# Linear attention with a feed-forward layer: the numerators' state part as 32x32 tiles, and the fourth denominators in the next group

## The reference

```python
def step(carry, qkv_t):
    kv_s, k_s = carry
    q_t, k_t, v_t = qkv_t
    kv_s = kv_s + jnp.einsum('bhe,bhf->bhef', k_t, v_t)
    k_s = k_s + k_t
    num = jnp.einsum('bhe,bhef->bhf', q_t, kv_s)
    den = jnp.einsum('bhe,bhe->bh', q_t, k_s)[..., None] + EPS_DEN
    return ((kv_s, k_s), num / den)
...
h = _layernorm(x, axis=-1) * (1 + ca) + sa
x = x + ga * _L0_attn_ref(h, L0_attn_W_qkv, L0_attn_b_qkv, L0_attn_W_out, L0_attn_b_out)
h = _layernorm(x, axis=-1) * (1 + cb) + sb
x = x + gb * _L0_ffn_ref(h, L0_ffn_w_gate, L0_ffn_w_up, L0_ffn_w_down)
```

## Time and profile before

| | us |
|---|---|
| median of 3 runs | 2108.07 |
| lowest, highest | 2107.64, 2109.33 |
| the profiled execution | 2109.39 |
| span of its instructions | 2107.6 |
| mean granted TensorE clock | 0.994 |

### The profile page before, as it was taken

How to read it: one execution, slowest core, us unless ns; L and a number is a source line. 1 busy time by engine, 2 the same in 40 slices (tenths; PEclk the granted TensorE clock), 3 DMA queues, 4 the chain that set the end, 5 groups by cost and what they waited for, 6 DMA issues and landing times. The chain is left out here.

```text
span 2107.6 us, 41310 instructions
## 1 busy us (share of the span) xinstructions
PE 2055.4 (98%) x14832; PEld 1669.0 (79%) x14832; DVE 1581.5 (75%) x2152; ACT 1006.0 (48%) x1733; POOL 991.0 (47%) x790
## 2 busy tenths in 40 slices
PE   5999999999999999999989999999999999999999
PEld 4788888888888888888868878788887888878787
DVE  7988988989989889889785674757557575674744
ACT  5444454455544555444434643535455354643533
POOL 2635545555454465544454344444434444344444
PEclk9999999999999999999999999999999999999999
DMA  7011122221232222222156465554656546465543
GB/s 254 31 52 58 65 86 86 96 91 56 78 99 81 91 68 79 86 81 80 65 171 229 153 220 170 193 181 145 209 179 199 179 153 211 153 219 170 168 157 109
DMA packets 157150, 276.60 MB, mean 131 GB/s; under 512 B 11105, under 2 KB 35681, under 8 KB 157026
## 3 DMA queue, kind: packets, MB, share of 16 engines
q1 hardware_dynamic: 156498, 273.73, 39.4%
q10 hardware_dynamic: 528, 1.05, 0.1%
HBM read 208.67 MB, written 66.06 MB: 130 GB/s over the span
## 5 line engine op out<-in xcount | busy, mean ns | idle before, releaser
L1429 POOL TENSOR_TENSOR h_lo<-y_rows,h_hi 128x512 fp32r<-128x512 f32 x192 | 246.7, 1304 | 406.9 <-ACT h_hi L1530 406.9
L424 POOL TENSOR_TENSOR x_res<-y,x_res 128x512 f32<-128x512 f32 x64 | 82.2, 1284 | 302.0 <-DVE y L843 302.0
L820 DVE RECIPROCAL r_den<-r_den 128x512 f32<-128x512 f32 x64 | 213.7, 3340 | 0.0
L582 ACT ACTIVATE z_exp<-pj,qk_neg 128x512 f32<-128x512 f32 x128 | 88.2, 689 | 213.9 <-PE pj L1073 186.6
L1073 PE MATMUL pj<-xt_hi,w_hi 128*128 128x512 f32 x512 | 151.0, 416 | 8.7 <-ACT xt_hi L574 4.2
L825 DVE TENSOR_TENSOR probs<-sc,causal 128x512 f32<-128x512 f32 x256 | 158.3, 678 | 1.3 <-PE sc L1101 1.3
L1836 PE MATMUL sc<-wd,h_hi 128*128 128x512 f32 x384 | 151.9, 396 | 5.7 <-DVE y L1666 5.7
L1836 PE MATMUL sc<-wd,h_lo 128*128 128x512 f32 x384 | 149.7, 390 | 0.0
L1642 DVE TENSOR_TENSOR r_den<-pj,k_tok 128x512 f32<-128x512 f32 x96 | 66.2, 689 | 103.5 <-ACT k_tok L1513 54.6
L1073 PE MATMUL pj<-xt_lo,w_hi 128*128 128x512 f32 x512 | 140.2, 396 | 0.9 <-DVE xt_lo L792 0.9
L1073 PE MATMUL pj<-xt_hi,w_lo 128*128 128x512 f32 x512 | 138.3, 392 | 0.0
(11 more groups left out here) (252 smaller groups left out, 5643.9 us busy)
## 6 DMA issues: line engine op xcount, KB each, us to landing
w_hi<-parts SPq DMA_DIRECT2D x48, 1024.0 KB, 5.2
w_lo<-parts SPq DMA_DIRECT2D x48, 1024.0 KB, 5.2
x_mid<-x_res SPq DMA_DIRECT2D x96, 256.0 KB, 2.1
x_res<-in_L_attn_x SPq DMA_DIRECT2D x64, 256.0 KB, 3.0
xg<-in_L_attn_x SPq DMA_DIRECT2D x15, 1024.0 KB, 6.9
x_res<-x_mid SPq DMA_DIRECT2D x60, 256.0 KB, 3.8
full<-x_mid SPq DMA_DIRECT2D x60, 256.0 KB, 3.3
parts<-r_den SPq DMA_DIRECT2D x48, 256.0 KB, 2.3
```

The lines of the kernel that those rows point to most:

```text
L424: pool.tensor_tensor(out=x_res[:, slot, :], in0=y[:, :], in1=x_res[:, slot, :], op=ALU.add).then_inc(y_ready, 1)
L582: act.activation(z_exp[:, n % 2, :], pj[:, n % 2, :], ACT.Relu, bias=qk_neg[:, 1 - kind, c:c + 1], scale=-scale).then_inc(below_ready, 1)
L820: dve.reciprocal(r_den[parity][:, c, :], r_den[parity][:, c, :]).then_inc(rden_ready, 1)
L1429: pool.tensor_tensor(out=h_lo[b], in0=h[i], in1=h_hi[b].bitcast(F32), op=ALU.subtract).then_inc(h_lo_ready, 1)
```

## The change

Three things change.

1. The state part becomes 16 products of 32x32, one for each head and block, which read only the nonzero blocks. The tile's row position is its head's partitions. Even blocks write their own head's partitions of `num`; odd blocks write one head further, in another bank: a bank of `sc` already masked (bank 3 in tiles 0 and 1, bank 2 in tiles 2 and 3, bank 0 in the last group). The V part writes to the same places. The division is two instructions of half width, one from each bank. Features of odd blocks so lie one head further from here on: the denominators use a second matrix `head_ones[:, 1, :]`, and the rows of W_out are put in the same order on the host.
2. The next group's denominator 3 no longer stands in tile 3 behind the numerators, but in the next group, between the first and the second projection unit of tile 0. ACT's copy of it goes behind the first `exp_relu`, and the vector engine's reciprocal behind the first `feature`. Denominator 1 moves ahead of the output projection in tile 2. In group 14 denominator 3 stands at the end of tile 3.
3. The waits follow: the scores wait for the division of the tile before, the numerators for the masks and copies of the bank that they borrow.

```diff
+    def odd_scores(tile, t):
+        return 0 if isinstance(tile, int) and tile >= (NG - 1) * GT else (3, 3, 2, 2)[t]
+    def num_part(tile, t, c, h):
+        to = (h + c % 2) % HPC
+        bank = sc[:, odd_scores(tile, t), :] if c % 2 else num
+        return bank[to * E:(to + 1) * E, c * P:(c + 1) * P]
...
             if ahead:
                 exp_relu(n, 0)
+                if not isinstance(g, int) or g > 0:
+                    den_out(g, parity, 3, den_bank)
                 exp_relu(n, 1)
...
-                exp_relu(n, 7)
                 if not isinstance(g, int):
                     act.wait_ge(down_out, g * 16 + (-16))
                 den_out(n, other, 1, den_bank)
+                exp_relu(n, 7)
...
-            if ahead:
-                den_out(n, other, 3, den_bank)
             if two_ahead:
                 xt_full(g + 2, 3, x_bank)
                 xt_high(g + 2, parity, 3)
+            if isinstance(g, int) and g == NG - 2:
+                den_out(n, other, 3, den_bank)
...
-            dve.tensor_tensor(out=a_t[:, :].rearrange("p (c i) -> p c i", c=C),
-                              in0=num[:, :].rearrange("p (c i) -> p c i", c=C),
-                              in1=r_den[parity][:, :, t * P:(t + 1) * P], op=ALU.mult).then_inc(a_ready, 1)
+            for odd, bank in enumerate((num, sc[:, odd_scores(tile, t), :])):
+                ins = dve.tensor_tensor(out=a_t[:, :].rearrange("p (k e i) -> p e k i", e=2, k=2)[:, odd, :, :],
+                                        in0=bank[:, :].rearrange("p (k e i) -> p e k i", e=2, k=2)[:, odd, :, :],
...
+            ins.then_inc(a_ready, 1)
...
             mask(g * GT)
+            if ahead:
+                feature(n, other, 0)
             recip(g, parity, 3)
-            if ahead:
-                feature(n, other, 0)
...
             wait(pe, y_gated, tile - 1)
+            wait(pe, a_ready, tile)
             wait(pe, ktok_ready, tile)
...
             wait(pe, kv_ready, tile)
-            wait(pe, a_ready, tile)
+            wait(pe, probs_ready, tile * HPC + odd_scores(tile, t) + 1)
+            if t >= 2 and (not isinstance(g, int) or g + 1 < NG):
+                wait(pe, den_ready, (g + 1) * C + t)
             for c in range(C):
-                pe.matmul(num[:, c * P:(c + 1) * P], kv_diag[:, c, :], qt[parity][:, c, t * P:(t + 1) * P],
-                          start=(c == 0), stop=False, skip_group_check=True)
+                for h in range(HPC):
+                    rows = slice(h * E, (h + 1) * E)
+                    pe.matmul(num_part(tile, t, c, h), kv_diag[rows, c, rows], qt[parity][rows, c, t * P:(t + 1) * P],
+                              start=(c < 2), stop=False, skip_group_check=True)
...
             if ahead:
                 project(g + 1, 1 - parity, 3 * t)
+                if t == 0 and (not isinstance(g, int) or g > 0):
+                    wait(pe, probs_ready, g * GT * HPC + 3)
+                    denominators(g, 3, den_bank)
                 project(g + 1, 1 - parity, 3 * t + 1)
...
-            if t == 3 and ahead:
+            if t >= 2 and ahead:
                 wait(pe, probs_ready, tile * HPC + 3)
-                denominators(g + 1, 2, den_bank)
+                denominators(g + 1, t - 1, den_bank)
...
-            if t == 3 and ahead:
-                denominators(g + 1, 3, den_bank)
...
+            if isinstance(g, int) and g == NG - 2 and t == 3:
+                pe.wait_ge(a_ready, tile + 1)
+                denominators(g + 1, 3, den_bank)
```

More of the change, by code:

```diff
@@ L124, in build @@
         causal = sbuf(top, "causal", [P, P])
-        head_diag = sbuf(top, "head_diag", [P, P])
-        head_ones = sbuf(top, "head_ones", [P, P], F32R)
+        head_ones = sbuf(top, "head_ones", [P, 2, P], F32R)
         c_col = sbuf(top, "c_col", [P, C])
@@ L876, in vector @@
         dve.memset(half_neg[:, :], -0.5)
-        link(dve.memset(head_diag[:, :], 0.0))
-        for h in range(HPC):
-            ins = dve.memset(head_diag[h * E:(h + 1) * E, h * E:(h + 1) * E], 1.0)
+        same_head = junk[:, 0:2 * P].rearrange("p (e n) -> p e n", e=2)
+        link(dve.memset(same_head, 0.0))
+        for odd in range(2):
+            for h in range(HPC):
+                to = (h + odd) % HPC
+                ins = dve.memset(same_head[h * E:(h + 1) * E, odd, to * E:(to + 1) * E], 1.0)
         link(ins)
-        dve.tensor_copy(head_ones[:, :], head_diag[:, :])
+        link(dve.tensor_copy(head_ones[:, :, :], same_head))
         dve.memset(ones[:, :], 1.0)
@@ L956, in group @@
                 dve.wait_ge(beyond_ps, 1)
-                dve.tensor_scalar(wide[:, :], x_bank[0:1, 0:1], 0.5, None, ALU.is_gt).then_inc(wide_ready, 1)
+                dve.tensor_scalar(wide[:, :], den_bank[0:1, 0:1], 0.5, None, ALU.is_gt).then_inc(wide_ready, 1)
             if ahead:
@@ L1079, in denominators @@
             wait(pe, den_ready, g * C + c)
-            pe.matmul(bank, head_ones[:, :], prod_hi[:, :], start=True, stop=False)
-            pe.matmul(bank, head_ones[:, :], prod_lo[:, :], start=False, stop=True).then_inc(den_ps, 1)
+            pe.matmul(bank, head_ones[:, c % 2, :], prod_hi[:, :], start=True, stop=False)
+            pe.matmul(bank, head_ones[:, c % 2, :], prod_lo[:, :], start=False, stop=True).then_inc(den_ps, 1)
         def scores(tile, g, parity, t):
@@ L1087, in scores @@
             wait(pe, y_gated, tile - 1)
+            wait(pe, a_ready, tile)
             wait(pe, ktok_ready, tile)
-            if not isinstance(g, int) or g + 1 < NG:
-                wait(pe, den_ready, (g + 1) * C + (0, 0, 1, 2)[t])
+            if not isinstance(g, int) or g > 0:
+                if not isinstance(g, int) or g + 1 < NG:
+                    wait(pe, den_ready, (g + 1) * C + t - 1)
+                else:
+                    pe.wait_ge(den_ready, NG * C)
+            else:
+                pe.wait_ge(den_ready, C + max(t - 1, 0))
             if isinstance(tile, int) and tile == (NG - 2) * GT + 1:
@@ L1124, in numerators @@
                     f = c * P + h * E
-                    mm = pe.matmul(num[h * E:(h + 1) * E, c * P:(c + 1) * P], v[parity][:, t, f:f + E],
-                                   probs[:, h, c * P:(c + 1) * P], start=False, stop=(c == C - 1),
+                    mm = pe.matmul(num_part(tile, t, c, h), v[parity][:, t, f:f + E],
+                                   probs[:, h, c * P:(c + 1) * P], start=False, stop=(c >= 2),
                                    skip_group_check=True)
@@ L1203, in rest @@
                 out_project(tile - 1)
-            if t in (1, 2) and ahead:
+            if t == 1 and ahead:
                 wait(pe, probs_ready, tile * HPC + 3)
-                denominators(g + 1, t - 1, den_bank)
+                denominators(g + 1, 0, den_bank)
             if t >= 2 and (not isinstance(g, int) or g + 2 <= NG):
@@ L1214, in rest @@
                 pe.wait_ge(probs_ready, (tile + 1) * HPC)
-                pe.matmul(x_bank[0:1, 0:1], beyond[:, :], ones[:, :], start=True, stop=True).then_inc(beyond_ps, 1)
+                pe.wait_ge(den_ready, (NG - 1) * C)
+                pe.matmul(den_bank[0:1, 0:1], beyond[:, :], ones[:, :], start=True, stop=True).then_inc(beyond_ps, 1)
             if isinstance(tile, int) and tile == 0:
@@ L1941 @@
             a = a.reshape(C, P)
+        if name == "L0_attn_W_out":
+            a = a.reshape(C // 2, 2, HPC, E, D)
+            a = np.stack([a[:, 0], np.roll(a[:, 1], 1, axis=1)], axis=1).reshape(D, D)
         layouts = [(f"in_{name}", a.T if name in _TURNED else a)]
```

9 lines of the change are left out of this document (6 added, 3 removed).

## The result

The changed kernel takes 2140.69 us, the median of four executions (2137.93 to 2142.56), the kernel before on the same chip 2108.23. The ratio is 1.0153, with an interval from 1.0141 to 1.0165: slower by 32.5 us. The forecast was 2140. Of all executions behind this document one, of `e8_full_matmuls`, stands apart (2548.70 us at a mean granted clock of 0.754, where its five others have 0.995 to 0.997); the numbers leave it out.

The account below looks back on a forecast made before the run. TensorE, busy for 98% of the span, was taken as the bound. Terms of -18.6, +2.2, -8.0, +36.7, +2.1 and +0.4 made +14.8 us, the clock +17, together +32: 2140 us against the median 2108.07, range 2110 to 2155.

Parts of the forecast that it names:

- State part: Numerators' state part as 32x32 tiles: four bursts, 0.69 us instead of 0.98, -18.6 us over 64 tiles.
- (c): State part: the two blocks of small tiles don't overlap, 2169 us, or in part 2150; chance 0.09.
- (d): State part: row tiles queue for the PSUM bank, +1.1 us a tile, 2229 us; chance 0.03.
- V part: Numerators' V part: columns turned by one head for odd blocks make bursts start later, 0.035 us a tile, +2.2 us.
- Fourth denominator out of tile 3: Between V part and x transposes in tile 3: 0.57 us saved a group, -8.0 us over 14 groups.
- The wait: Moved denominator in next group's tile 0 waits 2.5 us for the third mask: +2.62 a group, +36.7 us.
- Second denominator: Ahead of tile 2's output projection: waits about 0.15 us for the third mask, +2.1 us over 14 groups.
- Sum without the clock: Whole kernel: all terms except the falls of the granted clock sum to +14.8 us.
- The last group: Last group's waits for divisions and for the copy of the last denominator ahead of the first scores: +0.4 us once.
- The clock: Behind the denominator's stop: the granted clock falls in 10 of 14 groups, 1.7 us each, +17 us.
- Rival (b): Border: vector engine ahead of GpSimd, wait 1.7 us, clock holds, shape changes free: 2099 us; chance of faster 0.10.

Follow-up runs that it names:

- e8_full_matmuls: Kernel before, with the fourth denominator moved behind the next group's first unit and, except for the last group, the third reciprocal behind the masks: 2100.34 us.
- e1_move_alone: Kernel before, with only the fourth denominator, its copy and its reciprocal moved behind the next group's first unit, no small tiles: 2156.96 us.
- e6_tiles_one_bank: Kernel before, with the state part as 32x32 tiles in their natural places, both feature blocks in bank `num`: 2113.28 us, ratio 1.0029.

## Why the prediction was right, step by step

**State part: right.** Priced at 0.69 instead of 0.98, four bursts and two changes of shape; measured 0.59 and 0.10 ahead (scores to state part in tile 1 is 10.40 us for 10.30). -0.29, as said. The rivals on its size, (c) and (d), are out: no burst of one block waited for the other, and no row tile for its bank.

**V part: the term should have been nothing.** I took +0.035 us a tile for the turned columns. The V part's starts span 0.808 us as before; 2.2 us of the sum were not there.

**Fourth denominator out of tile 3: right.** V part to the next scores was 5.27 us and is 4.76 (741.33 to 746.10): -0.51, forecast -0.57. The prediction said itself that the transposes then meet the change of shape, and yet booked the pair's 0.57 in full; the transposes now take 0.41 to the next unit (742.35 to 742.76) where the trace before has 0.36.

**The wait: right, a little short.** 2.67 from slot to start, forecast 2.5. The choice between 2.75 and 1.7 hung on whether GpSimd holds up the low part of x. It does: the earlier start bought nothing, and the 39 low parts of the trace before would have told so ahead of the result. Had I followed the row all the way, the wait would have been 2.75; 2.5 gave the other case some weight. From slot to output projection +2.81 instead of +2.62, 14 groups +39.3.

**Second denominator: right.** 0.2 a group against 0.15.

**Sum without the clock.** A group where the clock holds: 66.08 us (the mean of the four such groups from 343 us on) less 64.73, +1.35; my terms made +1.18. The difference is the wait (+0.19), the fourth denominator's smaller gain (+0.06), tile 2 (+0.05) and the V part (-0.14). 14 x 1.35 = 18.9, less 0.27 for each of the eight tiles outside these groups, 16.7; the kernel with the filled stop measured 16.4 over before. The forecast was 14.8.

**The last group: about nothing, where 0.4 was priced.** Its first scores wait 0.50 us for the copy of the last denominator, and later ones 1.84 and 0.63 for divisions. But the output projections that waited before wait less, and its last state part starts 33.61 us behind its first scores, before 33.55.

**The clock: right in kind and sum.** Ten falls at 1.7 us forecast, nine at 1.6 measured, 14.4 by the groups' rows and 16.1 by the filled stop. So half of the 32.5 us is the wait, net of the gains, and half the clock behind it; the filled stop shows this, as it takes away the one and keeps the other.

**What stays open.** Why the clock fell in 9 groups of one kernel and in 13 of the other, with idle times of 2.44 to 2.57 us in the one and 2.45 to 2.52 in the other, and why behind 1.84 us it fell twice and held twice. The single falls show in the profiled executions only, one of each kernel; the mean granted clocks of the others (0.987 to 0.989, and 0.986 to 0.987 for `e1_move_alone`) say that they lost about as much. I guessed the number from two stops, and that it came out near was partly luck: 13 would have made 2147, still in the range. Rival (b) took a wait of 1.7 us as short enough for the clock; that is not safe, as a stop of 1.84 idle lost it.

**Rival (b)** asked for a vector engine ahead of GpSimd. The runs show where the faster kernel lies instead: not in a faster chain but in its order. Moving one reciprocal of 3.34 us from ahead of the masks to behind them took out the whole wait, the one for `v` too, and the clock's loss.

## What to carry to other kernels

Before you move a step behind an engine's wait, find the resource that it writes and ask when the last reader of that lets go, on the engine that is late at that very place; here a bank of four heads' scores was the wait, and a reciprocal that nobody needed soon stood ahead of its masks. Where TensorE is the bound, a stop of two microseconds or so can cost twice, by itself and by the clock behind it, so look first for something on the late engine that can change places. And cutting a matmul into small tiles need not pay by itself: here it lost 5.1 us with all blocks in their natural places, and was worth 13.5 with every other block shifted by one head and in a second bank.

## What the runs showed of the hardware

- **Row tiles share a bank.** The Trainium skill, "TensorEngine Tiling (Array Packing)", section "Restrictions and Gotchas", says that different row tiles can't access the same PSUM bank at once. By this case's rows they can where each has its own quarter of the partitions: four small tiles in `num` and four in `sc` start from 740.74 to 740.76, the next eight at 740.87 to 740.90. In one bank alone (`e6_tiles_one_bank`) it is a burst of four every 0.11 us as well (32 records in 1.01 us), the pace of full matmuls. Two different row tiles into the same quarter of one bank were not tried.
- **Blocks on the same small tiles and in the same bank queue**: 1.01 us, against 0.59 for blocks shifted by one and in two banks, both with the change of shape behind them. Whether tile or bank makes them queue was not parted.
- **A change from full matmuls to 32x32 tiles costs 0.10 us ahead** (from the k transposes to the state part 0.53 us, before 0.43), and 0.2 lie between the last burst and the V part, about what the earlier trace rows gave for the other change of shape.
- **The vector engine's subtraction ends with GpSimd's operation.** The low part of x takes 0.68 us alone (743.16, between the divisions and `v`), 1.32 and 1.80 beside GpSimd's 1.3 us addition, and ended 0.54 behind that addition in both kernels, though it started earlier in one.
- **Matmuls of no use hold the clock.** Ten in a stop of 2.67 us, and the granted clock stayed 1.00 in 14 of 14 groups, for 16.1 us; stops of 0.7 and 0.6 us cost no clock without them.
- **A stop of 1.84 us idle lost the granted clock in two profiled executions and kept it in two**, at the same place of the last group; idle times of 2.44 to 2.57 us lost it in 9 of 14 groups, of 2.45 to 2.52 in 13 of 14.
